# A Mamba block's gate: Silu four times per turn on two tiles, in place of twice on four

## The reference

```
h = layernorm(x) * (1 + scale) + shift ; h = h[:, perm]
xm, z = split(h @ W_in)                   # 1024 channels each
xm = silu(conv(xm)) ; dtr, B, C = split(xm @ W_xp)
dt = softplus(dtr @ W_dt + b_dt)
hst = hst * exp(dt * A) + dt * x * B      # over time, for 16 states
y = sum(hst * C) + xm * D
y = y * silu(z)                           # the gate
x + gate * (y @ W_out)[:, inv_perm]
```

## Time and profile before

| | us |
|---|---|
| median of 3 runs | 3052.7 |
| lowest and highest | 3052.64, 3056.3 |
| the profiled execution | 3057.33 |
| its span | 3055.3 |
| PE busy | 2685.9 (88%) |
| DVE busy | 2371.4 (78%) |
| POOL busy | 1875.2 (61%) |
| ACT busy | 1604.5 (53%) |

### The profile page before, as it was taken

One profiled execution on the slowest core, in us unless ns is written; L12 is line 12 of the kernel. 1 busy time (PEld: TensorE's weight loads), 2 busy tenths in 40 slices (PEclk: granted clock), 3 DMA queues, 4 the chain that ended last, 5 costly groups with the idle time before them and its releaser, 6 DMA issues. The chain is left out here.

```text
span 3055.3 us, 32727 instructions
## 1 busy us (share of the span) xinstructions
PE 2685.9 (88%) x11066; PEld 1532.6 (50%) x11066; DVE 2371.4 (78%) x3070; ACT 1604.5 (53%) x2412; POOL 1875.2 (61%) x822
## 2 busy tenths in 40 slices
PE   7999999999999877978988988888898897897974
PEld 3556466466465344554454454455455454455542
DVE  3455454554554489999999999999998998999993
ACT  1222223123222475875775776676677687587550
POOL 0111211221222087888899799799799799889991
PEclk9999999999999977999989999999998999998976
DMA  6012022212214434455675575575566566566653
GB/s 212 7 42 90 28 104 78 102 55 89 89 56 145 126 90 103 101 125 113 153 159 120 142 158 120 134 165 128 126 159 143 119 153 143 124 144 143 161 129 73
DMA packets 261596, 355.29 MB, mean 116 GB/s; under 512 B 21597, under 2 KB 115937, under 8 KB 261434
## 3 DMA queue, kind: packets, MB, share of 16 engines
q1 hardware_dynamic: 202200, 246.46, 26.2%
q0 software_dynamic: 55680, 105.93, 19.9%
q10 hardware_dynamic: 3554, 0.88, 0.1%
HBM read 215.56 MB, written 71.58 MB: 94 GB/s over the span
## 5 line engine op out<-in xcount | busy, mean ns | idle before, releaser
L1959 POOL TENSOR_TENSOR hs<-slots,b_wide 128x2048 f32<-128x2048 f32 x255 | 1267.5, 5000 | 146.9 <-PE bank L1487 142.7
L2146 DVE TENSOR_TENSOR_SCAN hs<-bank,hs 128x512 f32<-128x512 f32 x1024 | 1218.8, 1208 | 29.6 <-ACT bank L1732 23.8
L1732 ACT ACTIVATE bank<-dt,decay 128x512 f32<-128x512 f32 x1022 | 698.9, 691 | 543.6 <-DVE hs L2146 541.0
L1487 PE MATMUL bank<-ident,hs 128*128 128x128 f32 x4096 | 675.7, 294 | 248.9 <-DVE acc L2164 184.3
L1487 PEld LDWEIGHTS bank<-ident,hs 128*128 128x128 f32 x4096 | 513.4, 150 | 734.2 <-issue 265.8
L2164 DVE SCALAR_TENSOR_TENSOR acc<-bank,c_t,acc 128x512 f32<-128x512 f32 x772 | 561.2, 727 | 48.3 <-PE bank L1487 43.8
L1439 PE MATMUL bank<-h_t,w_in 128*128 128x512 f32 x1024 | 507.9, 605 | 1.6 <-ACT h_t L1652 1.6
L2007 POOL DMA_DIRECT2D acc<-scaled x252 | 288.5, 1145 | 48.4 <-DMA acc<-scaled 29.2
L1535 PE MATMUL bank<-w_y,zs 128*128 128x512 f32 x512 | 255.4, 605 | 1.3 <-DVE zs L2264 1.3
L1450 PE MATMUL bank<-w_out,h_in 128*128 128x512 f32 x448 | 221.5, 618 | 3.5 <-ACT dt L1699 3.5
L776 PE MATMUL bank<-z_t,w_k 128*128 128x512 f32 x512 | 221.2, 592 | 0.9 <-ACT z_t L875 0.9
(11 more groups left out here) (164 smaller groups left out, 3110.6 us busy)
## 6 DMA issues: line engine op xcount, KB each, us to landing
b_wide<-b_rows SPq DMA_DIRECT2D x256, 256.0 KB
acc<-scaled POOLq DMA_DIRECT2D x252, 256.0 KB
w_in<-in_L_cond_W_in SPq DMA_DIRECT2D x128, 256.0 KB, 4.4
z<-in_x SPq DMA_DIRECT2D x8, 2048.0 KB, 8.8
res<-in_x SPq DMA_DIRECT2D x8, 2048.0 KB, 9.8
h_tiles<-h_t SPq DMA_DIRECT2D x56, 256.0 KB, 2.8
h_in<-h_tiles SPq DMA_DIRECT2D x56, 256.0 KB, 5.2
x_rows<-w_part POOLq DMA_DIRECT2D x28, 512.0 KB, 6.7
```

The source lines that it names most:

```text
L1487: last = nc.tensor.transpose(bank[:, j * P:(j + 1) * P], hs[:, slot, j, t * P:(t + 1) * P], ident[:, :])
L1732: nc.scalar.activation(decay_banks[N % 3][:, :], dt[:, H % 2, j, :], ACT.Exp, scale=g.decay[:, 4 * (H % 2) + j, s:s + 1]).then_inc(da_read ...
L1959: nc.gpsimd.tensor_tensor(hs[:, U % RING, :, :], slots[:, H % SLOTS, :, :], b_wide[:, U % B_RING, :].unsqueeze(1).to_broadcast([P, 4, CHUNK]),
L2146: nc.vector.tensor_tensor_scan(block, decay_banks[N % 3][:, :], block, 0.0, ALU.mult, ALU.add).then_inc(scanned, 1)
```

## The change

`silu_z` takes a pair of tiles in place of a half of four. In turns 0 to 6 it stands at blocks 93, 104 and 110 and at block 2 of the next turn, in place of 104 and 2. In the last turn it stands at 60, 66, 72 and 78, in place of 66 and 78. Each call is followed by `exp_and_log_tables()` as before. The waits of the gate on DVE count pairs.

```diff
-SILU_Z_AT = (104, 2)
-LAST_SILU_Z_AT = (66, 78)
+SILU_Z_AT = (93, 104, 110, 2)
+LAST_SILU_Z_AT = (60, 66, 72, 78)
...
-            def silu_z(place, half):
-                for m in range(4 * half, 4 * half + 4)[-place.ring:]:
+            def silu_z(place, pair):
+                for m in (2 * pair, 2 * pair + 1):
                     need(act, *read_by(place, "z", m))
-                part = zs[:, 4 * half:4 * half + 4, :]
+                part = zs[:, 2 * pair:2 * pair + 2, :]
                 nc.scalar.activation(part, part, ACT.Silu).then_inc(zs_ready, 1)
...
-                    if n == SILU_Z_AT[1] and prev:
-                        silu_z(PLACES[b - 1], 1)
+                    if n == SILU_Z_AT[3] and prev:
+                        silu_z(PLACES[b - 1], 3)
                         exp_and_log_tables()
...
-                    if n == (SILU_Z_AT[0] if more else LAST_SILU_Z_AT[0]):
-                        silu_z(place, 0)
-                        exp_and_log_tables()
-                    if n == LAST_SILU_Z_AT[1] and not more:
-                        silu_z(place, 1)
-                        exp_and_log_tables()
+                    for pair, at in enumerate(SILU_Z_AT[:3] if more else LAST_SILU_Z_AT):
+                        if n == at:
+                            silu_z(place, pair)
+                            exp_and_log_tables()
...
-                need(dve, zs_ready, 2 * place.it + j // 4 + 1)
+                need(dve, zs_ready, KI // 2 * place.it + j // 2 + 1)
...
-                need(dve, zs_ready, 2 * BATCH)
+                need(dve, zs_ready, KI // 2 * BATCH)
```

More of the change, by code:

```diff
@@ L1903, in body @@
                             keep_z(place, m)
-                        silu_z(place, 0)
-                        silu_z(place, 1)
+                        for pair in range(KI // 2):
+                            silu_z(place, pair)
                 batches(act, body)
```

## The result

The changed kernel takes 3076.3 us (median of 6 runs, 3072.8 to 3091.5), the kernel before 3054.6 us beside it. The ratio is 1.0077, 95% interval 1.0065 to 1.0088: **0.77% slower**, +21.7 us. Measured once more among the experiments it was 1.0076 (1.0059 to 1.0093). The forecast was +19.0 us, 3071.7 us, range 3052 to 3088.

A forecast was written before the change was run, and what follows sets the result against it. DVE's scans bound the kernel overall, but ACT, PE and DVE are all full near block 93. Seven turns at 3.05 us give 21.4, less 2.4 in the last turn: +19.0 us, 3071.7 us, range 3052 to 3088.

The forecast's parts named there:

- Part 1: Cost on ACT of one two-tile Silu block with its table loads: 3.67 us; 5.6 us more ACT work per turn.
- Part 2: Block 93: scan 108 1.94 us late through decays; PE, DVE and POOL 2.4 us late through the copy of C.
- Part 3: After PE stands still at block 93, its clock may halve: 1.3 us per fall, 0.65 us taken per turn.
- Part 4: Block 110: the late start of the sum holds PE 2.3 us; DVE loses 1.2 us, from 0 to 2.5.
- Part 5: Block 2 of the next turn: the shorter Silu block gives 0.86 us back.
- Part 6: Block 19, turns 2 to 6: POOL, 2.4 us late, sets the time; with the clock 3.05 us per turn.
- Part 7: Last turn, blocks 60 to 78: shorter waits and less PE idling give -2.4 us, from -3.5 to -0.5.
- the signs in the prediction: PE idle 2.4 us behind block 91, 2.3 before y transposes; turns 0 to 6 longer by 2.4 to 3.7 us.
- (a): Faster: new blocks at 93 and 110 are covered, only the shortening counts: -14.5 us, 3038 us; chance 0.10.
- (b): No change: PE not held by the copy of C, POOL hides the rest: -2 to +6 us; chance 0.15.
- (c): Much slower: clock falls at 93 and 110 every turn, POOL hides nothing: +35 us, 3088 us; chance 0.13.
- (d): Silus of two pairs share one pair of table loads, so the change does less; chance 0.01.

The follow-up runs named there:

- the first half alone: Against the kernel before: Silus of z on two tiles at 93 and 104, four at next turn's 2, last turn unchanged; 3079.1 us, ratio 1.0080.
- the kernel with better places: Against the kernel before: four tiles at 104, two at 120, two at next turn's 2, last turn split as in the change; 3054.5 us, ratio 0.9998.
- the second half alone: Against the kernel before: four tiles at 104, two at 110, two at next turn's 2, last turn unchanged; 3066.6 us, ratio 1.0036.

## Why the prediction was right

The time was right, and so was the way of it at blocks 93 and 110. One step was wrong and several sizes were off, and they balance; that the difference of +19.0 came out within 3 us (5 in the second measurement) is partly luck.

- **Part 1**, the block of 3.67 us: 3.67 measured. No drain shows behind the loads. The Trainium skill, "ScalarE: Activation LUTs", section "What ACT_TABLE_LOAD costs", has 1.38 us more per switch; this trace does not agree, with 1.30 us from one start to the next.
- **Part 2**, block 93: forecast 1.1 us at scan 97, 2.4 at DVE's next sum, 1.94 at scan 108. Measured 1.12, 2.35 (at scan 98) and 1.75, where the clock holds. PE's wait for the copy of C was to be 2.4 us and is 2.29 in all seven turns. The chain Silu, copy of C, work bank, PE, DVE is as described. But the copy of C isn't needed for the loss: with it out of the way 1.78 us were lost through the decays. It matters for PE's clock: in the five profiles where PE waits for the copy the clock fell behind it in 21 of 35 turns, in the two where the Silu stands behind the copy in none of 14.
- **Part 3**, the clock: forecast 1.3 us for a fall, in half the turns. It fell in four turns in one profile and in one in another. At 93 a fall cost 1.33 us (3.08 against 1.75). Behind scan 108 it cost another 1.5, which part 4 had as its upper end (2.5) and the sum did not hold. Taken together 2.8 to 3.2 us for a turn with a fall in place of 1.3. This is the term that was mis-sized most.
- **Part 4**, block 110: forecast 1.2 us through the start of the sum; measured 1.46 where the clock holds. With the 0.2 us between scans 108 and 114, which I hadn't seen, a turn loses 3.45 us from 93 to 127 where 1.94 + 1.2 = 3.14 were worked out.
- **Part 5**, block 2: forecast 0.86 us back. Scan 6 is 0.76 us earlier, scan 7 0.86. How much of that lasts stays open. From block 0 to 93 the changed kernel won 3.7 us over turns 1 to 6, and 4.6 in its second profile. Of the kernels with an untouched block 2, the one with the last turn alone won 3.2 and the one with the first half alone lost 2.3. By the first comparison 0.1 or 0.2 us a turn was kept, by the second all of it; what unchanged blocks differ by between two executions is as large as the term. The times speak for little: the kernel with better places, whose block 2 is shorter, gained 1.1 us, and the last turn alone 4.0.
- **Part 6**, the account of POOL: the wrong step. I held that POOL's 2.4 us set the turn and that it would hide what DVE loses beyond it. The 3.45 us of blocks 93 to 127 were carried in full into the next turn: at scan 20 of turns 1 to 6 the changed kernel stands at -0.2, -0.1, 0.2, -1.1, -1.3 and 0.2 us, where the kernel with the last turn alone, which had lost nothing before, stands at 0.1, -0.2, 0.2, -1.1, -1.6 and 0.2. POOL does not hide such a loss, since it is made late itself: its waits for PE grew from 142.7 to 175.5 us. That POOL sets the time at block 19 and so hides a gain of DVE at the start of a turn fits these rows, but no run tests it by itself.
- **Part 7**, the last turn: forecast -2.4, measured -3.3 for the turn alone.

By these sizes the sum is 7 x 3.45 = 24.2, plus 2.9 for each fall, less 3.3 for the last turn: +20.9 with no fall, +23.8 with one and +32.5 with four, before anything that block 2 gives. The spans of the two profiled executions are 20.7 us (one fall) and 26.2 us (four falls) above that of the kernel before; the medians say +23.7 and +21.7. So the sum is 3 and 6 us too high for the two executions; the difference lies in the first layer and in the first 93 blocks of the turns, where also unchanged kernels differ.

The forecast of 3.05 us a turn was too low: turns 0 to 6 grew by 3.4 us on average in the profile with one fall and by 4.5 in the one with four. Of the signs in the prediction, those at blocks 93 and 110 came as told, but the lengths of the turns did not: from 1.9 to 6.6 us more in place of 2.4 to 3.7, with three of seven inside in each profile. Against that, the last turn was 4.1 and 4.4 us shorter by its last scan in place of 2.4, and the first scan of all came 2.2 and 1.9 us earlier, behind a layer that isn't touched.

Of the rivals, (a) fell: ACT hasn't 3.67 us between 93 and 104. (b) fell twice: PE was held by the copy of C, 2.29 us in each of seven turns, and with the copy out of the way POOL hid nothing (+15.5 us in place of -2 to +6). (c) is in part true of single turns, 6.3 us, but not of all seven. (d) didn't occur: the profile has 32 Silus and 32 loads ahead of them. The Trainium skill, "ScalarE: Activation LUTs", section "Table sets: the hidden batching unit", asks to batch by table set. The run without loads agrees: with the same cuts and no loads the kernel was not slower. But the batch is worth what the place says. A block with two more loads cost 0.01 us or less behind 120; at 94 it cost 1.78, although the shorter block at 104 gives 0.86 back.

## What to carry to other kernels

An engine with spare time on average can have none in the stretch where work is put: read its idle time between the new place and the next point that needs it (here 0.87 us for a block of 3.67), and then everything queued behind the block, small copies above all, since a copy of 0.2 us that frees a bank held another engine for 2.29 us. Count overheads that do not shrink when a piece of work is cut, here two table loads of 1.28 us for 1.06 us of Silu. Here a loss of DVE, the engine that bounds, was handed on in full by all that wait for it. A gain of 0.76 us at the start of a turn did not show in the times; before you count one, look for the next place where another engine is late anyway.

## What the runs showed of the hardware

A gap of 2.29 us on PE, in the same place of the same program, was followed by a fall of the granted clock in four of seven turns of one execution and in one of seven of another. In a kernel whose only difference is a Silu at 120 in place of 110 it was six of seven, twice the same ones, on two chips. A fall cost DVE 1.3 us by scan 108 in most turns, and 3.0 us in three, where the projections right behind the gap took 3.0 to 3.3 us in place of 1.98. At the other place, before the y transposes, a gap of 2.25 us was followed by a fall in four of seven turns of the kernel with the second half alone, and one of 2.26 us in none of seven of the kernel behind the copy of C. The length of a gap alone doesn't tell which; what does stays open.
